# DVE's order in the middle of a pass: the gates' chain first, both row maxima, then the residuals of y, and a coming pair's mean and variance at the pass's end

## The reference, cut to what matters

```python
x = x + layernorm(attention(layernorm(x)))      # 2 heads; half of each q and k is rotated by position
# attention: softmax(q k^T / 8) v, then @ Wo + bo
x = x + layernorm(ffn(layernorm(x)))
# ffn: base = x @ W.T; four low-rank experts (ranks 1, 2, 4, 8)
#   logits = l2norm(x @ Wp.T + bp) @ l2norm(sim) * exp(temp)
#   lw = softmax(logits); only the largest of the four is kept, as the gate of its expert
#   ffn = base + gate * (x @ Wd.T @ Wu.T)
```

## Time and profile before

| | us |
|---|---|
| median of 3 runs (lowest, highest) | 150.67 (150.66, 150.72) |
| the profiled execution's own time | 150.58 |
| its span, first to last instruction | 148.8 |
| busy: PE, DVE, ACT, POOL | 128.5 (86%), 130.7 (88%), 113.4 (76%), 87.3 (59%) |
| weight loads of PE | 106.0 (71%) |
| mean granted TensorE clock | 0.963 |

### The profile page before, as it was taken

The page is one execution under the profiler, slowest core; times in us unless marked ns, Lnnn a source line. Parts: engine busy times, 40 slices in busy tenths (PEclk is TensorE's granted clock), DMA queues, the critical chain, the costliest instruction groups (busy, mean ns, idle before and its releaser), DMA issues.

```text
span 148.8 us, 3110 instructions
## 1 busy us (share of the span) xinstructions
PE 128.5 (86%) x874; PEld 106.0 (71%) x874; DVE 130.7 (88%) x592; ACT 113.4 (76%) x378; POOL 87.3 (59%) x148
## 2 busy tenths in 40 slices
PE   0879799999999998999899989998999898965340
PEld 0467587988898788878887888797879776953220
DVE  6788879997988999899989998898889788899963
ACT  3657697969996989698969896989698958754460
POOL 6320826623846758676867686768545863338552
PEclk9999999999999999999999999999999999999555
DMA  3833250000000000100020002000200010000013
GB/s 74 209 98 92 74 134 5 4 0 0 7 0 2 0 0 4 70 0 2 4 73 0 0 0 75 0 0 0 73 4 2 9 62 0 4 0 2 0 70 141
DMA packets 5266, 4.83 MB, mean 32 GB/s; under 512 B 594, under 2 KB 5250, under 8 KB 5250
## 3 DMA queue, kind: packets, MB, share of 16 engines
q1 hardware_dynamic: 5104, 4.51, 10.4%
q10 hardware_dynamic: 146, 0.13, 0.3%
HBM read 2.54 MB, written 2.10 MB: 31 GB/s over the span
## 4 chain that ended last, share of the span: by engine, by line
PE 49%; DVE 27%; ACT 15%; issue 2%; POOL 2%; DMA 2%; POOLq 1%; DVEq 0%
PE ps_a L1372 6%; PE ps_s L1352 6%; ACT probs L438 6%; PE ps_z L1395 5%; PE ps_c L1372 4%; DVE neg_max L675 4%; PE ps_a L1362 4%; DVE x_all L695 3%; PE ps_b L1322 2%; PE ps_s L1383 2%; PE ps_s L1341 2%; PE ps_b L1362 2%; DVE y_all L688 2%; DMA x_all<-x 2%; PE ps_c L1341 2%
## 5 line engine op out<-in xcount | busy, mean ns | idle before, releaser
L438 ACT ACTIVATE probs<-ps_s,neg_max 128x256 f32<-128x256 f32 x60 | 25.3, 488 | 7.9 <-DVE neg_max L675 7.8
L675 DVE TENSOR_REDUCE neg_max<-ps_s 128x2 f32<-128x512 f32 x30 | 20.3, 680 | 0.6 <-PE ps_s L1352 0.4
L1352 PE MATMUL ps_s<-qk_t 64*128 64x256 f32 x120 | 17.0, 402 | 0.0
L1372 PE MATMUL ps_a<-v_all,probs_t 128*128 128x129 f32 x120 | 16.5, 280 | 0.0
L1372 PEld LDWEIGHTS ps_a<-v_all,probs_t 128*128 128x128 f32 x120 | 14.6, 191 | 2.0 <-issue 2.0
L1352 PEld LDWEIGHTS ps_s<-qk_t 64*128 64x128 f32 x120 | 10.3, 186 | 4.8 <-issue 4.0
L282 POOL TENSOR_TENSOR turn<-qk,sin_x 128x256 f32<-128x256 f32 x15 | 11.1, 740 | 3.1 <-ACT qk L424 2.2
L695 DVE SCALAR_TENSOR_TENSOR x_all<-y_all,rsy,x_all 128x128 f32<-128x128 f32 x32 | 11.8, 393 | 1.3 <-POOL rsy L297 0.7
L285 POOL TENSOR_TENSOR qk<-qk,cos_x 128x256 f32<-128x256 f32 x15 | 11.5, 767 | 1.2
L297 POOL TENSOR_TENSOR rsy<-var_y,power 128x4 f32<-128x4 f32 x6 | 6.5, 1078 | 9.3 <-ACT sq_y L449 9.3
L293 POOL TENSOR_TENSOR inv_norm<-norm,power 128x4 f32<-128x4 f32 x7 | 7.2, 1027 | 8.0 <-DVE norm L744 8.0
(11 more groups left out here) (342 smaller groups left out, 442.0 us busy)
## 6 DMA issues: line engine op xcount, KB each, us to landing
x_all<-x SPq DMA_DIRECT2D x7, 256.0 KB, 2.8
out<-x_all SPq DMA_DIRECT2D x7, 256.0 KB, 2.1
x_all<-x SPq DMA_DIRECT2D x2, 128.0 KB, 2.7
out<-x_all SPq DMA_DIRECT2D x2, 128.0 KB, 1.7
w_raw<-w_attn ACTq DMA_DIRECT2D x1, 128.0 KB, 2.8
w_raw<-w_attn SPq DMA_DIRECT2D x1, 128.0 KB, 2.9
bo_bp<-vectors SPq DMA_DIRECT2D x1, 80.0 KB, 3.5
ffn_raw<-w_ffn SPq DMA_DIRECT2D x1, 71.5 KB
```

Source lines behind the costliest of these rows:

```text
L438: last = act.activation(probs[:, u, j, :], scores_of(n, u)[:, j * T:(j + 1) * T], ACT.Exp, bias=neg_max[:, u, j:j + 1])
L675: dve.tensor_reduce(neg_max[:, u, :], scores_of(n, u)[:, :].rearrange("p (j k) -> p j k", j=TILES), AX.X, ALU.max, negate=True).then_inc(m ...
L1352: last = pe.matmul(scores_of(n, 2 * b + h)[:, j * T:(j + 1) * T], qk_t[r, b, 0, j * P:(j + 1) * P], qk_t[r, b, 1, :], start=True, stop=True)
L1372: last = pe.matmul(unit_of(n, u)[:, j * VW:(j + 1) * VW], probs_t[:, u, i, j * P:(j + 1) * P], v_all[:, at:at + VW], start=(i == 0), stop= ...
```

## The change

Four things are moved, nothing is added or removed but one wait. On DVE, in the loop over the passes: `logits` goes ahead of `keys`, and the rest of the gates' chain is drawn together between the four `stats`; `row_max` of units 2 and 3 stand one behind the other, with all residuals of y behind them (residual 1, 2 stood between the maxima, residual 3 behind the heads of unit 0); `mean` and `variance` of pair a + 3 leave the places between the gates and stand at the pass's end, before the second residual and `normalise`. `logits` gets a wait of its own for `below_top`, a result that is there. On ACT `expert_exps` goes ahead of the exponentials of unit 1. Lines behind 760 have one number more after the change.

```diff
@@ ACT, in the loop over the passes
                 if has(a - 1):
                     variance_y(a - 1, 1)
+                if done:
+                    expert_exps(a - 2)
                 if now:
                     exps(a, 1)
-                if done:
-                    expert_exps(a - 2)
                 if now:
                     probs_copy(a, 0)
@@ DVE
             def logits(n):
                 dve.wait_ge(inv_norm_ready, n + 1)
+                dve.wait_ge(route_link, n * 9 + 3)
@@ DVE, in the loop over the passes
                 if done:
+                    logits(a - 2)
                     keys(a - 2)
                 if has(a + 3):
                     stats(a + 3, 0)
                 if done:
                     top_key(a - 2)
-                    logits(a - 2)
-                    is_top(a - 2)
                 if has(a + 3):
                     stats(a + 3, 1)
+                if done:
+                    is_top(a - 2)
+                    shares(a - 2)
+                if has(a + 3):
                     stats(a + 3, 2)
                 if done:
-                    shares(a - 2)
                     pick(a - 2)
+                    sum_exps(a - 2)
                 if has(a + 3):
                     stats(a + 3, 3)
                 if done:
-                    sum_exps(a - 2)
+                    invert_sum(a - 2)
                 if last_:
                     residual_y(a - 1, 0)
                 if done:
-                    invert_sum(a - 2)
+                    gates(a - 2)
                 if has(a + 3):
                     gap(a + 3)
                 if done:
-                    gates(a - 2)
-                if has(a + 3):
-                    mean(a + 3)
-                if done:
                     gates_low(a - 2)
-                if has(a + 3):
-                    variance(a + 3)
                 if now:
                     row_max(a, 2)
+                    row_max(a, 3)
                 if last_:
                     residual_y(a - 1, 1)
                     residual_y(a - 1, 2)
-                if now:
-                    row_max(a, 3)
+                    residual_y(a - 1, 3)
+                if now:
                     weights_sum(a, 0)
...
                 if last_:
-                    residual_y(a - 1, 3)
                     stats_2(a - 1, 2)
...
                 if last_:
                     variance_2(a - 1)
+                if has(a + 3):
+                    mean(a + 3)
+                    variance(a + 3)
                 if done:
                     residual_z(a - 2, 0)
```

## The result

The kernel before takes 150.69 us in the median of 20 runs (150.5 to 150.81), the changed one 150.91 (150.72 to 151.0, 20 runs). The ratio is 1.0014, with a 95% interval of 1.0007 to 1.0020: 0.1 to 0.3 us slower. The profiled execution took 150.98 us (span 149.2, mean granted clock 0.965) against 150.58.

What follows compares the result with a forecast made beforehand. The prediction took TensorE's and ACT's order, not the nearly full DVE, to set the pace. Its terms, -0.21 + 0 + 0 + 0 + 0.43 = +0.22 us, took the median from 150.67 to 150.9 us, range 150.4 to 151.4.

Steps and rivals of the forecast that it cites:

- the floor of 14.84: Passes 2 to 4: pass length that TensorE's and ACT's order allows, read from pass 5, down from 14.91 us.
- Passes 2 to 4, -0.21 us: Mean and variance leave the middle, their two stalls go, and each pass falls from 14.91 to 14.84: 3 x 0.07.
- The expert exponential ahead, 0: ACT, five passes: expert exponential before unit 1's exponentials delays these by 0.19 us at most, without holding up TensorE: 0.
- The margin of 0.29 us: Time between the end of the row exponentials (65.23) and TensorE's scores that wait for them (65.52).
- Gates and maxima ahead, 0: DVE: both come earlier, but ACT's exponentials of unit 2 start by gated_copy, not by the maximum: 0.
- Mean and variance at the pass's end, 0 in passes 1 to 4: Three short DVE instructions, about 0.35 us a pass, covered by the 1.10 us freed or pass 1's wait for weigh: 0.
- Pass 0, +0.43: End of pass 0: mean, variance and a normalisation stall behind POOL's rotations, delaying turn_x(2) and pass 1's scores: +0.43 us.
- The 0.21 us that I let DVE gain: Pass 0: DVE's gain from 26.58 on, bringing it to the mean at 28.45, 0.04 behind POOL's rotation.
- A: Whole kernel: DVE is the bound and all of its stall comes back, -2.8 us in three passes, 147.9 us; chance 0.04.
- B: Pass 0: no collision with POOL, TensorE not held, only the -0.21 stays: 150.46 us; chance 0.2.
- C: ACT's wait for the logits delays TensorE's scores in each of five passes: about 151.5 us; chance 0.14.
- D: Pass 0 or 1: the change costs more than forecast, up to +0.65: 151.1 us or somewhat over; chance 0.15.

Runs made afterwards that it cites:

- the last kernel above: The changed kernel with pass 0's mean and variance back, ACT's copy of v before gated_t, and TensorE's turn_gated before weigh of unit 0: 149.2 us, ratio 0.9899.

## Why the prediction was right, and where it was not

The number held (150.9 against 150.91), and so did the two terms that made it, but one of them for a reason that the runs don't bear out; that its size came out right is luck as far as the named cause goes, and rests on the floor of 14.84 alone.

1. *Passes 2 to 4, -0.21 us.* The size was right: 0.25. The floor was right and is shown: passes stop at 14.83 in every version that gets there, and shortening ACT's stretch by one step lowered them to 14.57. The cause was named wrongly. I wrote that mean and variance leave the middle and their two stalls go, and gave the last residual's new place only as a reason why the residuals behind the maxima cost nothing. The runs say the reverse: moved alone, mean and variance cost 0.7 us, since a new stall arises at `normalise`, while the old one goes over to `gates_low`, where it costs nothing; put back into the changed kernel they cost nothing; and residual 3 alone gives the whole gain. The chain had it in its last line, TensorE at `turn_x2`; the timeline names the wait there, 0.6 us for `x_all`. I followed that chain back to DVE's longest pieces and took those for the cause, instead of asking what was the last thing that had to be done and whether it had to stand there.

2. *The expert exponential ahead, 0.* Right: undone, it is 1.0018 against 1.0014, and no wait for the exponentials stands at TensorE's scores in either. The margin of 0.29 us held (64.87 + 0.82 = 65.69 against 65.98). What the term left out is the other side: undone, it cost 0.1 us in pass 2, at `normalise`.

3. *Gates and maxima ahead, 0.* Right: maxima 0.9 us later and residuals between them cost nothing. But the room that the gates' chain makes on DVE is not without use. In the changed kernel `normalise(a + 2)` starts 0.39 us ahead of POOL's rotation and isn't caught; with the old order and mean and variance at the end it starts 0.27 or 0.28 ahead and is.

4. *Mean and variance at the pass's end, 0 in passes 1 to 4.* Right in the changed kernel, for which 0.35 us of DVE was the price that I took as covered. That the next instruction might be pushed into POOL's way, the very thing that I had worked out for pass 0, I looked for in no later pass. The cover is some 0.1 us wide, and with ACT's order undone it is gone in pass 2.

5. *Pass 0, +0.43.* Right in kind and nearly in size: +0.46 in the trace, and 0.35 + 0.22 = 0.57 between the medians of the two versions, 0.5 from the other side. The steps came as written: the mean ended with the first rotation, L655 slipped through, the variance ended with the second, one normalisation was held by the third, `turn_x` started 0.44 us later (0.27 without the late start; I had 0.31). The shares of the stalls were a little different, since DVE reached the mean 0.27 us behind the rotation and not 0.04. The 0.21 us that I let DVE gain there didn't come: a tiny instruction on the way, `sim_n<-sim_raw,sim_n` (L959), waited for the end of the rotation that POOL had in hand, in the kernel after from 26.63 to 27.06, against 26.31 + 0.73 = 27.04 on POOL; in the kernel before the same instruction had ended with the same rotation, at 26.88, so starting it earlier gains nothing.

6. *What was left out: pass 1.* The earlier trace rows were read only for the end of that pass. `turn_x2` waits for `x_all` there too, and the early residual gives 0.19 to 0.24 us in the versions that leave pass 0 alone. In the changed kernel 0.07 of it is left. DVE enters that pass late there, and TensorE's transposes of unit 3 start 0.58 us behind `turn_x2` (42.43 against 41.85) and not 0.47 as with pass 0 as before; but the version in which POOL waits gives back the same 0.07 after a pass 0 that isn't late, so this link isn't shown. The term that was left out hid itself in the sum, as the 0.1 us did that was lost behind the loop.

Of the rivals, A (DVE is the bound) is out: 0.49 us less DVE in pass 3 gave 0.07. By the Trainium skill, page "Perfetto Trace Analysis", section "Identifying the Most-Contended Engine", DVE would have been the engine to relieve; the runs don't agree here, since what was worth 1.2 us stood in an idle half microsecond of ACT, at 76% of the span. B is out, since the collision came. C is out. D didn't come: one normalisation was caught, not both, and nothing in pass 1.

What stays open: which part of the gates' new order makes the room before `normalise` was not tried, why pass 1 gives back only 0.07 us is argued and not shown, and the 0.1 us behind the loop was not followed.

## What to carry to other kernels

Follow a chain back to its last wait, and ask first whether the work that ends there could stand earlier in its engine's queue; the long pieces ahead of it may be movable at no gain. A stall behind another engine belongs to the place and the time, not to the instruction: moved away, it goes over to the next one, so for every moved instruction the distance of its followers from the other engine's next start has to be worked out, in each pass. And of two bounds that stand one behind the other the second one's size is what a repair of the first can't give; an idle engine inside that second stretch, here 0.5 us of ACT before a copy, is where a step of other work goes in free.

## What I had not expected of the hardware

The same first 15 us took different times in the profiled executions. The last matmul of 128x256 ahead of the first scores, and these, timeline of the kernel before, TensorE:

```profile
15.09 0.28 PE L1478 MATMUL ps_d<-w_low,xn_up 128*128 128x256 f32 x1
15.31 1.13 PE L1352 MATMUL ps_s<-qk_t 64*128 64x256 f32 x8
```

The same of the kernel after:

```profile
15.14 0.41 PE L1479 MATMUL ps_d<-w_low,xn_up 128*128 128x256 f32 x1
15.48 1.37 PE L1353 MATMUL ps_s<-qk_t 64*128 64x256 f32 x8
```

Before, one takes 0.28 us at 15.09; after, the same one still takes 0.41 at 15.14, and the scores take 1.37 instead of 1.13. The instructions and their order are the same up to there, and the granted clock reads 1.00 in that stretch in both, so the rows don't say why. What they do say is that there are two rates: the matmuls of 128x256 ahead of these start 0.21 us apart and take 0.41 each in both executions, and behind some moment they start 0.12 apart and take 0.28. That moment lies near 15 us in the kernel before and within the scores in the kernel after. In the 14 profiled executions of this case, all of kernels with the same instructions up to there, the first scores start between 15.06 and 15.51 us, so the spread is there without the change. From the second scores on (23.66 against 23.49) it moves everything by 0.17 us, which is most of the 0.22 us that was to be measured here: a difference of two single profiles has to be taken from a place behind it.

The width that decides on a stall is small. Two normalisations of 128x128 that started 0.39 us ahead of a rotation took 0.59 us, and 1.09 us when they started 0.27 or 0.28 ahead; their second starts some 0.26 us behind the first. At 0.32 ahead both came: 1.14 us in pass 2 of the kernel with ACT's order undone, 0.58 us in pass 2 of the last kernel above, where POOL's rotation took 0.86 us instead of 0.73.
